# A fast matrix algorithm's products in another order, with sums left to accumulate in PSUM

## The reference, cut to what matters

```python
# x (64, 64, 1024): per batch b a 64x64 matrix, chosen by condition[b], is applied
y = einsum('bct,bcd->bdt', x, weights[condition])      # the conditioned input, 4096 rows of 1024
scores = y @ Wr.T                                       # 64 experts
top_vals, top_idx = top_k(scores, 16); gates = softmax(top_vals)
G = zeros(N, 64); G[n, top_idx] = gates
h = einsum('nd,krd->nkr', y, A)                         # A: 64 x 16 x 1024
out = x + 2.0 * einsum('nkr,kdr->nd', h * G, B)         # B: 64 x 1024 x 16
```

## Time and profile before

| what | value |
|---|---|
| median of 3 runs | 763.11 us (762.77 to 764.93) |
| the profiled execution's own time | 764.61 us |
| its span, first to last instruction | 762.8 us |
| PE busy | 730.1 us, 96% |
| DVE busy | 532.6 us, 70% |
| ACT busy | 253.0 us, 33% |
| POOL busy | 376.3 us, 49% |
| chain that ended last | PE 71%, DVE 5%, ACT 1% |
| moved between DRAM and the core | 178.16 MB, mean 234 GB/s |

### The profile page before, as it was taken

One profiled execution on the slowest core, in us unless ns is written; L12 is line 12 of the kernel. 1 busy time (PEld: TensorE's weight loads), 2 busy tenths in 40 slices (PEclk: granted clock), 3 DMA queues, 4 the chain that ended last, 5 costly groups with the idle time before them and its releaser, 6 DMA issues.

```text
span 762.8 us, 9517 instructions
## 1 busy us (share of the span) xinstructions
PE 730.1 (96%) x3440; PEld 606.9 (80%) x3440; DVE 532.6 (70%) x913; ACT 253.0 (33%) x482; POOL 376.3 (49%) x250
## 2 busy tenths in 40 slices
PE   7998897699999999999999999999999999999998
PEld 6886675587888887888888887888888888787886
DVE  1449799999894378994455286996455266998564
ACT  3544462224442334213322244212323235230410
POOL 2664545959772073556083044728054126528272
PEclk9998899799999999999999999999999999999999
DMA  9928337647668677647676767566676868554673
GB/s 318 346 81 319 126 145 252 224 177 278 244 256 312 233 294 258 226 165 260 215 267 236 263 250 278 191 205 227 211 261 250 297 216 305 192 193 137 243 246 147
DMA packets 56720, 178.16 MB, mean 234 GB/s; under 512 B 10850, under 2 KB 10978, under 8 KB 56162
## 3 DMA queue, kind: packets, MB, share of 16 engines
q1 hardware_dynamic: 54658, 173.04, 62.9%
q10 hardware_dynamic: 2016, 4.52, 1.6%
HBM read 131.40 MB, written 46.14 MB: 233 GB/s over the span
## 4 chain that ended last, share of the span: by engine, by line
PE 71%; DVE 5%; ACT 1%; issue 0%; DVEq 0%
PE Pb L248 35%; PE Pb L231 26%; PE Cb L210 6%; PE S L263 3%; DVE Cq L342 1%; DVE Ox L170 1%; DVE Op L170 0%; ACT Ex L297 0%; ACT Cq L353 0%; DVE Q L342 0%; PE T L280 0%; PE T L332 0%; DVE s L310 0%; DVE s L303 0%; DVE m L292 0%
## 5 line engine op out<-in xcount | busy, mean ns | idle before, releaser
L231 PE MATMUL Pb<-Op,Wt 128*128 128x512 f32 x1056 | 255.8, 399 | 15.4 <-DVE Op L170 12.2
L231 PEld LDWEIGHTS Pb<-Op,Wt 128*128 128x128 f32 x1056 | 200.2, 192 | 61.0 <-DVE Op L170 12.5
L248 PE MATMUL Pb<-Wt,Op 128*128 128x512 f32 x912 | 216.8, 396 | 7.9 <-DVE Op L170 6.4
L248 PEld LDWEIGHTS Pb<-Wt,Op 128*128 128x128 f32 x912 | 171.4, 190 | 45.8 <-DVE Op L170 7.3
L342 POOL TENSOR_TENSOR Cq<-Cq 128x512 f32<-128x512 f32 x96 | 152.8, 1608 | 110.5 <-DVE Cq L342 54.8
L342 POOL TENSOR_TENSOR R<-R 128x512 f32<-128x512 f32 x64 | 94.9, 1501 | 141.7 <-DVE Op L170 125.7
L342 DVE TENSOR_TENSOR Q<-Pb,Q 128x512 f32<-128x512 f32 x128 | 85.1, 685 | 77.4 <-PE Pb L248 51.8
L342 POOL TENSOR_TENSOR Q<-Q,u 128x512 f32<-128x512 f32 x48 | 71.6, 1531 | 79.3 <-DVE u L342 79.3
L170 DVE TENSOR_TENSOR Op<-R,Op 128x512 fp32r<-128x512 f32 x104 | 91.2, 906 | 26.8 <-ACT Op L168 26.8
L248 PE MATMUL Pb<-Wt,Ox 128*128 128x512 f32 x432 | 100.8, 391 | 0.0
L248 PEld LDWEIGHTS Pb<-Wt,Ox 128*128 128x128 f32 x432 | 80.5, 188 | 16.3
(11 more groups left out here) (60 smaller groups left out, 466.8 us busy)
## 6 DMA issues: line engine op xcount, KB each, us to landing
Wt<-Wd SPq DMA_DIRECT2D x168, 512.0 KB, 4.5
Wd<-Wt SPq DMA_DIRECT2D x56, 512.0 KB, 3.4
Q<-in_x SPq DMA_DIRECT2D x32, 512.0 KB, 4.6
xc<-in_x SPq DMA_DIRECT2D x24, 512.0 KB, 3.9
out<-Q SPq DMA_DIRECT2D x32, 256.0 KB, 2.8
out<-Q SPq DMA_DIRECT2D x16, 512.0 KB, 2.9
BR<-in_B SPq DMA_DIRECT2D x3, 1024.0 KB, 8.3
Q<-in_A ACTq DMA_DIRECT2D x8, 256.0 KB, 7.7
```

The source lines that it names most:

```text
L231: t = pe.run(lambda e, c=c, o=o, a=a, z=z: e.matmul(Pb[:, b, :], Wt[:, k, a, 128 * c:128 * c + 128], part(o, z), start=(c, a, z) == (0, 0, ...
L248: t = pe.run(lambda e, c=c, o=o, k=k, a=a, z=z: e.matmul(Pb[:, b, :], part(o, a)[:, 128 * i:128 * i + 128], Wt[:, k, z, :], start=(c, a, z ...
```

## The change

Four things change together.

1. The order of the products is another, and some of them (`CHAIN`) start without clearing their bank, so that they add to what the product four steps before left in it. The bank is read after each of them. P5 adds to P1, P3 to that; P7 to P6, P4 to that; Q6 to Q1, Q7 to that; Q4 to that; Q3 to Q5. Each drain is now one read of the bank (P1: one copy and one add), and no drain uses GpSimd.
2. The sums change place with the order: T1 to T4 are sum_t1 to sum_t4, in another order in GpSimd's queue; S1 of the gated side gets a place of its own (`u`, in superblock 0 the place of `xc`); S1 to S4 of the A side stand in another order, and 12 of the 16 are written behind T1's four; of the five sums per c on the B side two stay on GpSimd, two are on VectorE, and one is gone.
3. A unit made from the third product on is first copied by ScalarE into a PSUM bank (`Cb`, or S and T), and VectorE's subtraction reads it there.
4. Operands have ten places in superblock 0: two in the memory of `xc` (`Xo`). Loads into `xc` for superblock 1 start at step 18 of the second phase (before: step 6), and Cb's units of superblock 1 are at steps 20 to 27 (before: every second step from 10 to 24).

The routing's places move too: `g_turn` of the first gates from (2, 3) to (2, 1), `top_b` and `top_c` from (2, 0), (2, 1) to (1, 3), (2, 0); the second `top_a`, `top_b`, `top_c` from (3, 1), (3, 2), (3, 3) to (3, 3), (4, 0), (4, 1).

```diff
-FIRST = ["P1", "P2", "P3", "P5", "P6", "P7", "P4"]
-SECOND = ["Q2", "Q4", "Q1", "Q5", "Q6", "Q7", "Q3"]
+FIRST = ["P2", "P1", "P5", "P3", "P6", "P7", "P4"]
+SECOND = ["Q2", "Q1", "Q6", "Q7", "Q4", "Q5", "Q3"]
+CHAIN = {"P5", "P3", "P7", "P4", "Q6", "Q7", "Q4", "Q3"}
...
+        Xo = sb("Xo", [128, 2, 2, 512], F32R)
...
-        op_free, op_spare = [None] * (NO + 4), deque(range(NO))
+        op_free, op_spare = [None] * (NO + 6), deque([*range(NO), NO + 4, NO + 5])
...
-        def unit(n, src, *tokens):
+        def unit(n, src, *tokens, free=None, bank=None):
...
+            if bank is not None:
+                ac.after(free[0], *tokens)
+                ac.run(lambda e: e.copy(bank, src), False)
             ac.after(w_free.get(n - NW), w_kept.get(n - NW), *tokens)
             hi = ac.run(lambda e: e.copy(Wt[:, k, 0, :], src))
             ve.after(hi)
-            lo = ve.run(lambda e: e.tensor_tensor(Wt[:, k, 1, :], src, f(Wt[:, k, 0, :]), ALU.subtract))
+            whole = src if bank is None else bank
+            lo = ve.run(lambda e: e.tensor_tensor(Wt[:, k, 1, :], whole, f(Wt[:, k, 0, :]), ALU.subtract))
+            if bank is not None:
+                free[0] = lo
...
-                        start=(c, a, z) == (0, 0, 0), stop=(c, a) == (3, 1)), a == 1 and (last or c == 3))
+                        start=fresh and (c, a, z) == (0, 0, 0), stop=(c, a) == (3, 1),
+                        skip_group_check=not fresh), a == 1 and (last or c == 3))
...
-            if name in ("P1", "P3", "P5"):
+            if name in ("P2", "P1", "P5", "P3"):
...
-                if name == "P5":
-                    t = Cq_ready[2][j] = add(ve, c[2], P, c[2], t, Cq_ready[2][j])
...
-            elif name == "P6":
-                t = Cq_ready[0][j] = add(ve, c[0], P, c[0], done, Cq_ready[0][j])
-                Cq_ready[2][j] = add(gp, c[2], c[2], c[0], t, Cq_ready[2][j])
-                Cq_ready[3][j] = add(gp, c[3], c[3], c[0], Cq_ready[3][j])
...
+                if name == "P1":
+                    t = Cq_ready[1][j] = add(ve, c[1], P, c[1], t, Cq_ready[1][j])
             else:
-                t = Cq_ready[0][j] = add(ve, c[0], P, c[0], Cq_ready[0][j], done)
+                q = {"P6": 2, "P7": 3, "P4": 0}[name]
+                t = Cq_ready[q][j] = add(ve, c[q], P, c[q], done, Cq_ready[q][j])
...
+            tile, e = {"Q2": (4 + i, 0), "Q1": (4 + i, 0), "Q6": (4 + i, 1), "Q7": (i, 1), "Q4": (i, 0), "Q5": (i, 1),
+                       "Q3": (4 + i, 1)}[name]
+            t = into(tile, e)
...
                         if m == 0:
-                            a_unit(1, j, an_ready[j][1])
-                            t = raw["S3", j] = add(gp, lo4, lo, lo4, an_ready[j][0], an_ready[4 + j][0],
-                                                   op=ALU.subtract)
...
+                            a_unit(1, j, an_ready[j][0])
+                            raw["S1", j] = add(gp, S1, A21, A22, an_ready[4 + j][0])
                         elif m == 1:
...
+                            a_unit(2, j, raw["S1", j])
+                            raw["S3", j] = add(gp, A21, A11, A21, raw["S1", j], an_ready[j][0], op=ALU.subtract)
+                            raw["S2", j] = add(gp, A11, S1, A11, raw["S3", j], made[1, j], op=ALU.subtract)
+                            raw["S4", j] = add(gp, A12, A12, A11, raw["S2", j], made[0, j], op=ALU.subtract)
...
                     if m == 0:
...
+                            need("y11", c)
+                        if s and j == 3:
+                            for c in range(4):
+                                sum_t1(c)
                     elif m == 1:
+                        for c in late[j]:
+                            need("T1", c)
+                    elif m == 2:
+                        for c in early[j]:
                             need("y22", c)
+                        sum_t2(j)
+                    elif m == 3:
+                        for c in ((0, 1, 2, 3), (), (), ())[j]:
                             need("y12", c)
+                        for c in late[j]:
+                            need("T2", c)
...
+                    if s == 0 and m < 6:
...
+                        t = unit(28 + 4 * (m + 1) + c, src, tok, free=(s_free, t_free)[c % 2],
+                                 bank=(S[:, :], Tf)[c % 2])
+                        if m == 0:
+                            raw["T2b", c] = add(ve, B11, B11, B12, t, raw["T3b", c])
+                        elif m == 1:
+                            raw["T4b", c] = add(ve, u[:, c, :], u[:, c, :], B11, raw["B21", c], raw["T2b", c],
+                                                op=ALU.subtract)
+                            raw["T1b", c] = add(gp, B11, B22, B11, t, raw["T4b", c], op=ALU.subtract)
...
                     if m == 0:
                         gated(0, c, 0)
-                        need("G22", c)
+                        need("G11", c)
+                        raw["S1g", c] = add(gp, s1_place(c), q[0], q[1], Cq_ready[0][c], Cq_ready[1][c],
+                                            u_busy[c] if s else xc_free[c // 2])
+                        Cq_ready[0][c] = add(gp, q[0], q[3], q[0], Cq_ready[3][c], raw["S1g", c], op=ALU.subtract)
+                        Cq_ready[3][c] = add(gp, q[3], s1_place(c), q[3], Cq_ready[0][c], split["G11"][c][1],
+                                             op=ALU.subtract)
```

More of the change, by code:

```diff
@@ L237, in first, with second @@
             return b, t
-        def second(n, ops, i, last):
+        def second(n, ops, i, last, fresh):
             b = bank_n[0] % 4
@@ L384, in store @@
                     of[128 * (n + tile):128 * (n + tile) + 128, lo:hi], Q[:, tile, lo:hi]))
[L386 to L395, removed]
-            elif name == "Q5":
[L397 to L410, removed]
+            tile, e = {"Q2": (4 + i, 0), "Q1": (4 + i, 0), "Q6": (4 + i, 1), "Q7": (i, 1), "Q4": (i, 0), "Q5": (i, 1),
+                       "Q3": (4 + i, 1)}[name]
+            t = into(tile, e)
+            if name == "Q1":
+                store(tile, 0, 512, t)
+            elif name == "Q5":
+                store(tile, 0, 1024, t)
+            elif name == "Q3":
+                store(tile, 512, 1024, t)
             bank_free[b] = t
-        Cq_busy = [[None] * 4 for _ in range(4)]
+        Cq_busy = [[()] * 4 for _ in range(4)]
         def cond_weights(s, half):
@@ L533, in pool_t4, with sum_t1, sum_t2 @@
-            def pool_t4(c):
-                t4[c] = add(gp, R[:, 0, 4 + c, :], R[:, 0, 4 + c, :], R[:, 1, 4 + c, :], split["y21"][c][1], t2[c],
-                            op=ALU.subtract)
+            y11, y21, y12, y22 = [[R[:, k // 2, 4 * (k % 2) + c, :] for c in range(4)] for k in range(4)]
+            def sum_t1(c):
+                t1[c] = add(gp, y11[c], y12[c], y11[c], split["y11"][c][1], R_ready[1][0], op=ALU.subtract)
+            def sum_t2(c):
+                t2[c] = add(gp, y11[c], y22[c], y11[c], split["T1"][c][1], R_ready[1][1], op=ALU.subtract)
@@ L537, in need, with sum_t3, sum_t4, s1_place @@
+            def sum_t3(c):
+                t3[c] = add(gp, y12[c], y22[c], y12[c], split["y12"][c][1], R_ready[1][1], op=ALU.subtract)
+            def sum_t4(c):
+                t4[c] = add(gp, y21[c], y21[c], y11[c], split["y21"][c][1], t2[c], op=ALU.subtract)
+            def s1_place(c):
+                return u[:, c, :] if s else S1x[c]
             def need(name, c):
                 src, tok = {
-                    "y11": (R[:, 0, c, :], None), "y21": (R[:, 0, 4 + c, :], R_ready[0][1]),
@@ L547, in need @@
                 split.setdefault(name, []).append(operand(src, tok))
[L549 removed]
+            uses = ["y21", "y11", "T1", "y22", "T2", "T3", "T4"]
+            early, late = ((0, 1), (2,), (3,), ()), ((), (0,), (1,), (2, 3))
             state = {}
@@ L723, in adaln_ffn @@
-                    if s == 0 and step in (6, 8):
-                        load_x(1, step // 2 - 3)
-                    b, done = second(base + 28 + 4 * m, split[uses[m]], i, i == 3)
-                    if more and (step in range(10, 26, 2) if s == 0 else step in range(2, 24, 3)):
-                        k = step // 2 - 5 if s == 0 else step // 3
-                        for a in range(2):
+                    elif m < 6:
+                        need(uses[m + 1], c)
+                        if m == 4:
+                            (u_busy if s else S1_split)[c] = split["S1"][c][1]
+                    elif more:
+                        split.setdefault("next", []).append(operand(y21[c], R_ready[0][1]))
@@ L729, in adaln_ffn @@
+                    if s == 0 and step in (18, 20):
+                        xc_free[(step - 18) // 2] = S1_split[step - 17]
+                        load_x(1, (step - 18) // 2)
+                    b, done = second(base + 28 + 4 * m, split[uses[m]], i, i == 3, name not in CHAIN)
+                    if more and (step >= 20 if s == 0 else step in range(2, 24, 3)):
```

(2 more changed lines are left out.)

247 lines of the change are left out of this document (94 added, 153 removed).

## The result

The changed kernel takes 786.74 us (784.41 to 790.53, 4 runs), the kernel before 764.02 us (762.77 to 765.27, 4 runs) beside it: ratio 1.0302, interval 1.0256 to 1.0348. It is slower by 22.7 us, where 754.2 was forecast. The profiled execution took 786.6 us and its span is 784.5.

The account below looks back on a forecast made before the run. PE bound the kernel, with 37.3 us to be had in superblock 0, where VectorE was late. Superblock 0 at 232.2, the rest plus 1.0, gave a 753.9 span; 1.8 outside it, less 1.5 to the median: 754.2 us, range 741 to 762.

Parts of the forecast that it names:

- the early gates become the bound, in every superblock: Rival, chance 0.10: in superblocks 1 to 3 the turn waits 3.7 us plus 3.2 of clock each, so 774 us.
- the one for superblocks 1 to 3: Gates ready 11.1 us after the scores' turn at (2,1), 11.8 at (4,2), PE there at 10.9: waits 0.3 and 0.9.
- the 0.87 that went as forecast: Superblocks 1 to 3: PE's old wait for VectorE, 0.87 us in each, was to go.
- (2,0) and (2,1): Superblock 0: PE idle 3.8 + 1.1 us at (2,0) for T1's splits, then 3.7 at the first gates' turn at (2,1).
- The clock behind them: Superblock 0, after the waits at (2,0) and (2,1): matmuls at the low clock lose 5.3 us.
- (4,2): Superblock 0: top_c in (4,1) makes the gates' turn after (4,2) wait 1.0 us.
- VectorE needs four instructions a step, 2.4 us against PE's 2.73: Superblock 0, from (3,0) to the first phase's end: VectorE's work per step is below PE's; phase ends at 131.8 us.
- Second phase: Superblock 0: PE idle 1.4 + 4.6 us for G11 and 1.1 for S2, plus 2.2 of clock, sum 9.3.
- Cb's tiles: Superblock 0, steps 20 to 27: loads of xc land in 3.8 to 6.9 us, mostly covered; PE loses 0.5 us.
- GpSimd and VectorE at one port: VectorE instructions with both inputs in SBUF wait for GpSimd's one in flight; a pair costs 1.7 us, GpSimd some 0.45 late.
- The second rival: Chance 0.25: VectorE mostly gets in first at the shared port, GpSimd waits; 731 us, or 742.6 if half vanishes.
- The detour through a bank: Superblock 0: 44 ScalarE copies at 0.6 us stay off the path; their splits take 0.60 instead of up to 1.71.

Follow-up runs that it names:

- e14: Changed kernel, early turns kept, with only VectorE's add and maxima on the scores issued right behind the scores' turn: 768.54 us, ratio 1.0051 to the kernel before.
- e8: e7 with the exponentials of both turns, in every superblock, issued behind the casts of the following step: 753.02 us, ratio 0.9845 to the kernel before.
- e11: e1 with at most one weight load per step in the last product of superblock 0: 757.70 us, ratio 0.9909 to the kernel before.
- e5: e1 with its 44 late units split straight from SBUF, without the copy into a bank: 764.50 us, ratio 1.0009 to the kernel before.
- e13: Kernel before with only its 28 B-side units in superblock 0 copied by ScalarE into a bank and split there: 760.73 us against 764.73, ratio 0.9927.
- e1: Changed kernel with the gates' turns moved later, the first to (2,3), the second to (4,3): 760.91 us, ratio 0.9957 to the kernel before.
- e7: e1 with the second gates' turn at (5,0) and the gating that needs it one step later: 756.92 us, ratio 0.9902 to the kernel before.

## Why the prediction was wrong

The rival that I gave 0.10, "the early gates become the bound, in every superblock", is what happened: it said 6.9 us per superblock, and the trace has 6.3, 7.8 and 8.3. That the sizes are so near is partly luck, since it had one wait of 3.7 with 3.2 of clock where there are two, 2.04 and 3.24, with 1.9 to 3.5 of clock. The range reached to 762 and left it out. Of the 30.6 us by which the span was missed (753.9 forecast, 784.5 measured), 21.3 lie in superblocks 1 to 3 (1.0 forecast, 22.3 measured) and 9.3 in superblock 0 (9.9 gained by forecast, 0.6 measured); the rival's 774 kept the gain in superblock 0.

- **The step that failed** is the one for superblocks 1 to 3: 11.1 us from the scores' turn to the gates at (2,1), 11.8 at (4,2), against PE's 10.9. PE's side was right. Measured are 13.0 and, by 307.62 - 293.47, 14.1. That is 1.9 and 2.3 us too few. By its size, what the two figures left out is what stands between the turn of the scores and `top_a`: P1's add, which waits for ScalarE's copy, and a split (2.2 us), and at the second turn a copy, a cast and two splits (3.07 us). e14 takes just that out of the chain and gets 11.3 and 11.9 us, the forecast's own figures within 0.2, and the waits shrink by 1.6 and 2.3. The exponentials ahead of the next copy are in e14 too, so they aren't the step that failed; outside superblock 0 (e8) their price is not shown. The prediction gives 11.1 and 11.8 without their terms, so more can't be said of how they came about.
- **A small miss, a large price.** 4.2 us too few per superblock became 6.3 to 8.3: 5.3 idle where 1.2 was forecast, another 1.9 to 3.5 of low clock that I had priced for superblock 0 but not for superblocks 1 to 3, less the 0.87 that went as forecast.
- **(2,0) and (2,1):** 3.8 + 1.1 forecast, 3.82 measured and no second one; 3.7 forecast for the first turn, 3.14 measured. The first two are right in place and nearly in size. The clock behind them was forecast at 5.3 and came to some 3: 12 matmuls took 3.34 and 2.67 us where 12 take 3.0.
- **(4,2):** 1.0 forecast, 6.29 measured, with low clock behind it: the largest miss in superblock 0. The first phase ends at 137.80 us, 131.8 was forecast. "VectorE needs four instructions a step, 2.4 us against PE's 2.73" counts its work; it was busy 20.44 of the 27.10 us from 82.90 to 110.00 and still late. The trace has the same kind of thing ahead of `top_a` (98.44 us: two splits of 2.75 us together beside GpSimd's sums, 5.2 us behind the turn) and ahead of `top_b` (2.65 us idle for the cast of a unit). e14 took back only 1.2 of the 6.29, so for the rest the cause is read and not shown.
- **Second phase:** 1.4 + 4.6 + 1.1 forecast for G11 and S2, 1.87 + 4.35 + 1.66 measured, and 2.2 of low clock forecast, 2.4 measured (48 matmuls in 13.45 us, 11.04 at 2.4 GHz): right.
- **Cb's tiles:** 0.5 forecast; 1.90 idle. The tile queued behind loads of weights in SP's queue (e11); I had taken 3.8 to 6.9 us of landing from the earlier trace rows, where those loads were not ahead of it. It took up to 9.0.
- **The start:** step (0,1) starts at 28.75 us, before at 27.17 (a wait of 1.31 us for WrT, and low clock). No run ties this to the change.
- **GpSimd and VectorE at one port:** right in place. The second rival (VectorE keeps ahead) did not happen: sums and splits within SBUF still take 1.49 us and 0.90 in the second phase. The Trainium skill (SBUF — State Buffer, who interferes with whom) lets issue order decide; here both pay, VectorE more: its sums a mean of 1.49 for 0.68 us, GpSimd's adds a mean of 1.60 for 1.27.
- **The detour through a bank** was worth 4 us, in both kernels (e5, e13). The fixed part of 120 cycles that the Trainium skill gives a bank as source (VectorE: DVE Perf Modes, the section on the TRN2 errata) doesn't show: the splits from S and T took 680 and 685 ns, and those from R, within SBUF, 684 in the kernel before in the same stretch.

## What to carry to other kernels

When a small serial chain (here scores to gates) runs through engines that also drain a matmul's banks, don't sum its own instructions: write down, from the trigger to the release, what stands ahead of each of its instructions in each queue, and count every hand-over to the other engine with what that engine does first. If the margin to the consumer comes out under a microsecond or two, take the consumer a step later: that cost nothing here (e1, e7), and idle gaps of 2 to 3 us on PE cost up to 1.7 us more each in clock. And ask of each load what else its queue issues in the same step.

## What the runs showed of the hardware

- A gap of 2.04 us on PE was followed by full clock in superblock 1 (24 matmuls in 5.72 us) and by a stretch at the low one in superblock 2 (7.30), with the same instructions around it: the same gap costs nothing or 1.6 us.
- ScalarE's copy from SBUF into a bank, which no row of before had, took 0.59 us for 128x512. The forecast's 0.6 held:

```profile
L191 ACT COPY S<-BR 128x512 f32<-128x512 f32 x9 | 5.3, 592 | 16.1 <-DVE Wt L196 16.1
```

- VectorE's busy time fell by 81.5 us and GpSimd's by 145.7 with the change, and with the turns put back the kernel gained 3.9 us of 764.8.
- What stays open: why the wait at the fifth step of the second phase (4.1 to 4.4 us in e1, e7 and e8) doesn't shrink with any of the edits but that of the B sums, and what the accumulation in banks would be worth under another order.
